# Forming 4-bit feed-forward weights during the attention, from gathered table rows

## The reference, cut to what matters

```python
def _dequant(qweight, scales, qzeros, g_idx):
    shifts = jnp.arange(PACK, dtype=jnp.uint32) * BITS            # PACK 8, BITS 4
    qw = qweight.astype(jnp.uint32)
    w = (qw[:, None, :] >> shifts[None, :, None] & MAXQ).reshape(-1, qweight.shape[1])
    qz = qzeros.astype(jnp.uint32)
    z = ((qz[:, :, None] >> shifts[None, None, :] & MAXQ) + 1).reshape(qzeros.shape[0], -1)
    s = scales[g_idx]
    return (w.astype(scales.dtype) - z[g_idx].astype(scales.dtype)) * s
Wg = _dequant(gate_qweight, ...)     # 512 x 1376, 4 groups
Wu = _dequant(up_qweight, ...)       # 512 x 1376, 4 groups
Wd = _dequant(down_qweight, ...)     # 1376 x 512, 10 groups
h = jax.nn.silu(xf @ Wg) * (xf @ Wu)
out = h @ Wd
```

## Time and profile before

| | us |
|---|---|
| median of 3 runs | 1183.19 (1180.73 to 1184.94) |
| the profiled execution, its time | 1182.78 |
| its span in the profile | 1181.0 |
| TensorE busy | 1121.7 (95%) |
| VectorE busy | 751.9 (64%) |
| ScalarE busy | 541.7 (46%) |
| GpSimd busy | 416.3 (35%) |

### The profile page before, as it was taken

One profiled execution on the slowest core, in us unless ns is written; L12 is line 12 of the kernel. 1 busy time (PEld: TensorE's weight loads), 2 busy tenths in 40 slices (PEclk: granted clock), 3 DMA queues, 4 the chain that ended last, 5 costly groups with the idle time before them and its releaser, 6 DMA issues. The chain is left out here.

```text
span 1181.0 us, 19222 instructions
## 1 busy us (share of the span) xinstructions
PE 1121.7 (95%) x6643; PEld 959.8 (81%) x6643; DVE 751.9 (64%) x1572; ACT 541.7 (46%) x1437; POOL 416.3 (35%) x421
## 2 busy tenths in 40 slices
PE   4899999999999999999999998789999999988998
PEld 3798998998998998998998887657768777676877
DVE  6555555555555555555555677789874566789863
ACT  4445445445445445445445454333332445465631
POOL 4442332332332332332332442144431333485521
PEclk9999999999999999999999999999999999999999
DMA  6211011011011011011010020023212225244300
GB/s 213 77 36 33 23 37 32 24 37 32 24 36 32 23 37 32 24 37 32 24 30 11 1 70 1 9 63 81 81 47 54 63 49 121 72 90 99 80 11 36
DMA packets 48716, 56.49 MB, mean 48 GB/s; under 512 B 10822, under 2 KB 29270, under 8 KB 48620
## 3 DMA queue, kind: packets, MB, share of 16 engines
q1 hardware_dynamic: 48620, 55.26, 17.3%
HBM read 40.56 MB, written 2.10 MB: 36 GB/s over the span
## 5 line engine op out<-in xcount | busy, mean ns | idle before, releaser
L379 PE MATMUL bank<-wqkv,kvT 128*128 128x256 f32 x1536 | 201.3, 288 | 8.7 <-DVE vv L567 8.7
L424 PE MATMUL bank<-wo,aoT 128*128 128x512 f32 x768 | 193.6, 401 | 5.6 <-DVE acc L563 5.6
L379 PEld LDWEIGHTS bank<-wqkv,kvT 128*128 128x128 f32 x1536 | 189.5, 193 | 10.4 <-DVE vv L567 10.4
L367 PE MATMUL bank<-wqkv,kvT 128*128 128x512 f32 x768 | 188.8, 395 | 1.7 <-DVE qn L577 1.7
L424 PEld LDWEIGHTS bank<-wo,aoT 128*128 128x128 f32 x768 | 140.6, 190 | 33.8 <-DVE aoT L558 6.3
L367 PEld LDWEIGHTS bank<-wqkv,kvT 128*128 128x128 f32 x768 | 141.7, 191 | 28.9 <-issue 1.8
L663 POOL TENSOR_TENSOR rms<-msq,half_neg 128x4 f32<-128x4 f32 x64 | 64.5, 1008 | 220.5 <-DVE msq L574 220.3
L666 POOL TENSOR_TENSOR rms<-msq,half_neg 128x2 f32<-128x2 f32 x64 | 44.6, 697 | 133.5 <-DVE msq L583 133.5
L550 ACT ACTIVATE prob<-bank,nmax 128x128 f32<-128x128 f32 x256 | 90.3, 372 | 2.1 <-DVE nmax L587 2.1
L875 PE MATMUL bank<-x2T,wgu 128*128 128x512 f32 (+1 forms) x336 | 90.3, 413 | 0.0
L528 ACT ACTIVATE qsq<-bank 128x512 f32<-128x512 f32 x64 | 38.2, 597 | 112.8 <-PE bank L367 112.8
(11 more groups left out here) (181 smaller groups left out, 2203.8 us busy)
## 6 DMA issues: line engine op xcount, KB each, us to landing
wqkv_raw<-in_L_xattn_Wq_dram SPq DMA_DIRECT2D x32, 256.0 KB, 2.5
wo_raw<-in_L_xattn_Wo_dram SPq DMA_DIRECT2D x32, 256.0 KB, 2.7
qS<-qhl SPq DMA_DIRECT2D x32, 256.0 KB, 3.7
kS<-chl SPq DMA_DIRECT2D x32, 128.0 KB, 3.1
packed<-_L_ffn_gate_qweight_dram SPq DMA_DIRECT2D x40, 64.0 KB, 2.3
packed<-in_L_ffn_up_qweight_dram SPq DMA_DIRECT2D x40, 64.0 KB, 2.3
packed<-_L_ffn_down_qweight_dram SPq DMA_DIRECT2D x10, 256.0 KB
acc<-in_x_dram SPq DMA_DIRECT2D x8, 256.0 KB, 5.7
```

What stands on the lines that cost most here:

```text
L367: mm = pe.matmul(b_q[:, :], kvT[:, l, kt, p, 1:3, :], wqkv[:, par, r, kt, 0:QW], start=(kt == 0 and n == 0), stop=(kt == KT - 1 and n == 2))
L379: mm = pe.matmul(b_kv[:, b * 256:(b + 1) * 256], kvT[:, l, kt, p, 2 * b:2 * b + 2, :], wqkv[:, par, r, kt, QW:QKV], start=(kt == 0 and n = ...
L424: mm = pe.matmul(b_o[:, :], aoT[:, l, h, :, :], wo[:, par, r, h, :], start=(h == 0 and n == 0), stop=(h == G - 1 and n == 2))
```

## The change

It takes dequantization out of the feed-forward part. Tables of zeros and scales are put together in DRAM (`sp_tables`, and the first three steps of `dve_between`): a row of `table[k, b]` has the zeros plus one and behind them the scales of one group, for up to 512 columns. The weights are cut into 35 chunks, [128 x 512] or [128 x 352] for gate and up and [128 x 512] for down. Each chunk is loaded by SP, with every packed row on 8 partitions; GpSimd gathers for each partition the table row of its group by an indirect DMA (`gather_row`, between the key power and `lo_piece`); VectorE forms the weights in three operations (`dequant`: shift and mask, subtract, multiply), in place; and SP stores them to DRAM. From step 5 on each step has two of these operations, one where `dve_between(..., "rq")` stands, between `msq` and `qn`, and one behind the step ("end").

In the feed-forward part a tile's weights are now loaded from DRAM (`weight_tile`, three tiles ahead), ScalarE makes the high part and VectorE (for tile 0 GpSimd) the low part, three operations of 512 columns each. The one-hot matrices, `spread`, the scale splits and everything that fed them are gone. The first products of the feed-forward part and the transposes of its input stand inside the last steps of the attention. Weight pieces of the attention are loaded in the same order as before, interleaved with the new loads and stores.

```diff
@@ sp_first
-            for g in range(1, KVH):
-                group(g)
-            sp_scales(sp)
-            wo_piece(KVH - 1, 3, 4 * KVH - 2)
+            qkv_piece(1, 0, 3)
+            wo_piece(0, 3, 2)
+            qkv_piece(1, 1, 4)
+            wo_piece(1, 0, 3)
+            sp_tables(sp)
+            for j in range(STEPS0 - 6):
+                sp_quantized(sp, j)
+                weight_load(j)
@@ pe_step0
+            if st.j == UNITS:
+                pe.wait_ge(s_qT, UNITS)
+                pe.wait_ge(s_kT, UNITS)
+                x2_transposes(pe, 0)
+                x2_transposes(pe, 1)
             if st.has(2, UNITS):
...
+            if st.j > UNITS and st.j < UNITS + 3:
+                inner_product(pe, 0, st.j - UNITS - 1)
             if st.has(3, UNITS):
...
+            if st.j == UNITS:
+                x2_transposes(pe, 2)
+                x2_transposes(pe, 3)
@@ dve_step0
                 dve.tensor_scalar(msq[:, 0:4], ssq[:, 0:4], 1.0 / HD, RMS_EPS, ALU.mult, ALU.add).then_inc(s_qms, 1)
+                dve_between(dve, st.j, "rq")
                 dve.wait_ge(s_rq, st.done(0))
@@ pool_step0
                 pool.tensor_tensor(rms[:, 4:6], msq[:, 4:6], half_neg[:, 4:6], ALU.pow).then_inc(s_rk, 1)
+            gather_row(pool, st.j)
             lo_piece(pool, st)
@@
+        FIRST = 5
+        BLOCKS = -(-F // D)
+        CHUNKS = 2 * KT * BLOCKS + FT
+        def weight_store(sp, c):
+            k, t, b, w, rows_, _ = chunk(c)
+            sp.wait_ge(s_deq, 3 * c + 3)
+            src = qch[0:rows_, c % 2, 0:w].bitcast(F32)
...
+        def sp_quantized(sp, j):
...
+            for c in range(CHUNKS):
+                if j == done_step(c) + 1 and c + 2 < CHUNKS:
+                    quantized_load(sp, c + 2)
+            for c in range(CHUNKS):
+                if j == done_step(c):
+                    weight_store(sp, c)
+        def done_step(c):
+            return FIRST + (3 * c + 2) // 2
+        def gather_row(pool, j):
+            for c in range(CHUNKS):
+                if j != (FIRST - 1 if c < 2 else done_step(c - 2)):
+                    continue
+                k, _, b, w, rows_, col = chunk(c)
...
+                if c >= 2:
+                    pool.wait_ge(s_deq, 3 * (c - 2) + 3)
+                pool.indirect_dma_start(rows[0:rows_, c % 2, 0:2 * w], None, table[k, b][:, :],
+                                        bass.IndirectOffsetOnAxis(idx[0:rows_, col:col + 1], 0)).then_inc(s_row[c % 2], 16)
@@ dve_between
+            if where in ("rq", "end"):
+                o = 2 * (j - FIRST) + (where == "end")
+                if 0 <= o < 3 * CHUNKS:
+                    dequant(dve, *divmod(o, 3))
+        def dequant(dve, c, step):
+            _, _, _, w, rows_, _ = chunk(c)
+            q = qch[0:rows_, c % 2, 0:w]
+            if step == 0:
...
+                dve.wait_ge(s_q_in[c % 2], 16 * (c // 2 + 1))
+                dve.tensor_scalar(q, q, shift[0:rows_, 0:1], 15, ALU.logical_shift_right, ALU.bitwise_and).then_inc(s_deq, 1)
+            elif step == 1:
+                dve.wait_ge(s_row[c % 2], 16 * (c // 2 + 1))
+                dve.wait_ge(s_deq, 3 * c + 1)
+                dve.tensor_tensor(q.bitcast(F32), q, rows[0:rows_, c % 2, 0:w], ALU.subtract).then_inc(s_deq, 1)
             else:
+                dve.wait_ge(s_deq, 3 * c + 2)
+                dve.tensor_tensor(q.bitcast(F32), q.bitcast(F32), rows[0:rows_, c % 2, w:2 * w], ALU.mult).then_inc(s_deq, 1)
@@ pe_ffn
             for n in range(FT + ALONE):
...
                 if n >= 1:
                     inner_product(pe, n, 0)
-                else:
-                    spread(pe, 1, (0, 1))
-                inner_product(pe, n, 1)
+                    inner_product(pe, n, 1)
@@ dve_ffn
                 if n + 1 < FT:
-                    dequant(dve, f + 1, (0, 1, 2))
+                    w_lo(dve, f + 1, (0, 1, 2) if n else (2,))
@@ sp_l1x
-            sp.wait_ge(s_zs, CHUNKS * FT)
+            sp.wait_ge(s_wqkv, 4 * KVH)
@@ the GpSimd block, ahead of the last step of ident
+            pool.memset(z_raw[:, :, :], 0).then_inc(s_blank, 1)
+            pool.memset(idx_raw[:, :], 0).then_inc(s_blank, 1)
+            pool.iota(pid[:, :], pattern=[[0, 1]], base=0, channel_multiplier=1).then_inc(s_pid, 1)
```

More of the change, by code:

```diff
@@ L703, in block_kernel @@
         f_d = bank[4:8]
[L704 to L707, removed]
+        FIRST = 5
+        WEIGHTS = (("gate", F, GG), ("up", F, GG), ("down", D, GD))
+        BLOCKS = -(-F // D)
+        CHUNKS = 2 * KT * BLOCKS + FT
+        z_line = [nc.dram_tensor(f"z_line_{m}", (g, n), F32).ap() for m, n, g in WEIGHTS]
+        w_gu = nc.dram_tensor("w_gu", (FT, P, 2, KT, P), F32).ap()
+        w_d = nc.dram_tensor("w_d", (F, D), F32).ap()
+        table = {(k, b): nc.dram_tensor(f"table_{m}_{b}", (g, 2 * min(D, n - b * D)), F32).ap()
+                 for k, (m, n, g) in enumerate(WEIGHTS) for b in range(-(-n // D))}
         ALONE = 3
         EVEN_DONE = UNITS - PAIRS
-        s_rest = sem("s_rest")
-        HALF_ZS, QUARTER_ZS = ZS // 2, ZS // 4
         X2 = 1
@@ L715, in width, with chunk @@
             return min(P, F - f * P)
-        def sp_scales(sp):
-            sp.wait_ge(s_zero, 1)
-            for m, at, n, g in TABLES:
-                for row in SCALE_ROWS:
-                    sp.dma_start(s_raw[row:row + g, at:at + n], a[f"L0_ffn_{m}_scales"]).then_inc(s_sraw, 16)
+        def chunk(c):
+            if c < 2 * KT * BLOCKS:
+                i, b = divmod(c, BLOCKS)
+                return i // KT, i % KT, b, min(D, F - b * D), P, i
+            f = c - 2 * KT * BLOCKS
+            return 2, f, 0, D, width(f), 2 * KT + f
@@ new lines, in stores, with stored, sp_tables @@
+        def stores(c):
+            return 1 + (c < 2 * KT * BLOCKS and c % BLOCKS == BLOCKS - 1)
+        def stored(c):
+            return 16 * sum(stores(b) for b in range(c % 2, c + 1, 2))
+        def sp_tables(sp):
+            sp.wait_ge(s_blank, 2)
+            for k, (m, n, g) in enumerate(WEIGHTS):
+                sp.dma_start(z_raw[0:g * n // 64, k, :], a[f"L0_ffn_{m}_qzeros"].rearrange("g c -> (g c)")
+                             .rearrange("(p c) -> p c", c=8)).then_inc(s_zraw, 16)
+                for b in range(-(-n // D)):
+                    w = min(D, n - b * D)
+                    sp.dma_start(table[k, b][:, w:2 * w], a[f"L0_ffn_{m}_scales"][:, b * D:b * D + w]).then_inc(s_tab, 16)
+            for k, m in enumerate(("gate", "up")):
+                sp.dma_start(idx_raw[:, k * KT:(k + 1) * KT],
+                             a[f"L0_ffn_{m}_g_idx"].rearrange("(t p) -> p t", p=P),
+                             allow_slow_non_contiguous=True).then_inc(s_idx, 16)
+            rest = F // P * P
+            sp.dma_start(idx_raw[:, 2 * KT:2 * KT + F // P],
+                         a["L0_ffn_down_g_idx"][0:rest].rearrange("(t p) -> p t", p=P),
+                         allow_slow_non_contiguous=True).then_inc(s_idx, 16)
+            sp.dma_start(idx_raw[0:F - rest, 2 * KT + F // P:2 * KT + FT],
+                         a["L0_ffn_down_g_idx"][rest:F].rearrange("(p o) -> p o", o=1)).then_inc(s_idx, 16)
@@ L858, in spread_next @@
-        def spread_next(pe, n, k):
-            if n + 1 < FT:
-                spread(pe, n + 1, (k,))
         def inner_product(pe, n, m):
@@ L900, in pe_ffn, with whole_down @@
         def pe_ffn(pe):
-            def whole_down(n, now):
-                down(pe, n, (0, 1))
-                spread_next(pe, now, 4)
-                down(pe, n, (2, 3)).then_inc(s_d, 1)
-                spread_next(pe, now, 5)
+            def whole_down(n):
+                down(pe, n, range(HP)).then_inc(s_d, 1)
             for n in range(FT + ALONE):
```

461 lines of the change are left out of this document (182 added, 279 removed).

## The result

The changed kernel takes 1142.88 us, the median of 4 runs (1142.49 to 1144.09), beside 1182.95 us (1180.73 to 1184.94) for the kernel before on the same chip. The ratio is 0.9662, with a 95% interval of 0.9646 to 0.9678. The forecast was 1146.0 us, in a range of 1138 to 1172. The profiled execution spans 1141.1 us, 39.9 less than the 1181.0 of before.

The account below looks back on a forecast made before the run. TensorE bounds attention without a gap; in FFN tiles table matmuls and waits for dequantization add 1.39 us to its 8.44. Sum: 1182.8 - 11.3 - 15.0 - 12.5 + 2.0 = 1146.0 us, range 1138 to 1172.

Parts of the forecast that it names:

- Attention's steps: Steps 5 to 57: the 105 new VectorE operations mostly fit idle time, 2.24 us at a step's end; cost 2 us.
- The rival of contention in every step: Attention: new operations meet GpSimd's low part and power every time, TensorE loses 0.5 us per step; 1170.5 us, chance 0.16.
- Table set-up: Steps 1 to 3 and before the first transpose: loads and 16 small VectorE operations lie in gaps; cost nothing.
- Steps 58 to 64: End of attention: zero tables, one-hots and scale splits of the old dequantization go; gain 11.3 us.
- Hand-over: Step 64's marker to tile 1's gate product: 23.5 us in place of 38.5; gain 15.0, ends 10 and 17.5.
- the spell at the lower clock: Hand-over: one spell of TensorE at a lower clock was expected to stay, 1.5 us of the 23.5.
- Tiles 1 to 10: FFN first half: only TensorE's 8.44 us per tile should bind, without the 1.39 us between; gain 12.5 us.
- The turn: Tile 10 to the second half of the FFN: the prediction had no term here, forecast change 0.
- The gather: 35 indirect DMAs on GpSimd in attention: about 4.2 us of GpSimd time free per gather, no loss taken.
- The 3.1 us that the prediction weighed against it: Gather: descriptors of a GpSimd DMA blocked by VectorE's two-port mode, from 620 to about 3100 ns; still below the threshold.
- the 7.5 us of the rival: Gather too long: query power late, then TensorE; loss above 4.2 us, break-even 6.4, at 7.5 us 1202; chance 0.11.

Follow-up runs that it names:

- the second of the edits: The changed kernel with the VectorE operation at the step's end moved ahead of the queries, in front of the square sums: 1141.99 us, ratio 0.9653.
- the trace at 4.0 us: The changed kernel with 9 chained small memsets behind each gather, so that GpSimd is held for 4.0 us: 1156.35 us, ratio 0.9761.
- 18 memsets: The changed kernel with 18 chained small memsets on GpSimd behind each gather, so that it is held for 7.2 us: 1238.38 us, ratio 1.0465.

## Why the prediction was right, and where it was not

The sum came out 3.1 us above the median: 39.9 us of span were gained, and 36.8 forecast. No single term made that difference. The two stretches missed by more than 2 us have opposite signs and nearly cancel; what is left is the hand-over, and a little of each of the others. That the sum came so close owes 2.5 us each way to luck.

**Attention's steps, +2.0 forecast, +1.33 measured.** The mechanism was the one named: the operation at the end is held by GpSimd's low part, and in a step without a gather the excess over the room reaches TensorE. 0.18 us per event was right (0.2). The number of events was not worked out; there are 6. Moving the operation away, the second of the edits above, removed the loss in every step. The rival of contention in every step, 1170.5 us, is excluded: 35 operations are stretched and 27 of them cost nothing.

By the rule of the Trainium skill that the prediction weighed ("SBUF — State Buffer", section "Who interferes with whom"), the two-input operations are held for the whole of GpSimd's instruction; the trace agrees, at 2.35 us. The prediction took the rule for two-input operations alone; line 1062, with one tensor input and a scalar per partition, was held in the same way, 2.10 us.

**Table set-up, nothing forecast, +2.1 measured.** This step failed. It was called a matter of gaps "of the same kind", and the step's end has room for 2.24 us; but in steps 1 and 2 the first of four small shifts was held by GpSimd's low part, 1.25 and 1.86 us in place of 0.17. The four took 1.49 and 2.09 us together, and TensorE waited 1.60 us for `vv` in place of 0.22, and in the next step 0.45 in place of nothing. The room at the end of an early step was not read from a row of that step; the rows were from 300 us on. The version with the set-up ahead of the queries has these 2.1 us back. Another 0.45 us are in the start before the first marker, which varies by more from run to run (41.5 to 43.7 us in the profiles here).

**Steps 58 to 64, -11.3 forecast, -11.6 measured.** As argued; no run takes this term apart.

**Hand-over, -15.0 forecast, -16.6 measured.** The windows of the kernel before and, in the second fence, of the changed one, over exactly this stretch:

```profile
745.65:784.14 38.49, 26.61 (x132) 20.37 (x131) 29.68 (x69) 12.99 (x32) 9.41 (x14) 0.91 0.11 28
```

```profile
737.93:759.81 21.88, 20.09 (x113) 16.90 (x112) 17.00 (x33) 12.56 (x28) 6.21 (x7) 1.00 0.12 37
```

TensorE's own work is 20.09 us, where the sum had 19.4. The wait for `qT` is 1.20, as forecast, and one more of 0.59 is left where the sum had 1.3; these two misses cancel. The term that failed is the spell at the lower clock, 1.5 us: the clock is 1.00 throughout, with stops of 1.20 and 0.59 us and no longer one. Before, TensorE stood idle for 11.9 us of the stretch, and the clock was 0.91 in it.

**Tiles 1 to 10, -12.5 forecast, -12.7 measured.** The first takes 8.98 us, with a wait of 0.41 for `hval`; the others take 8.35, a little less than the 8.44 that gate, up and down take in the earlier trace rows. VectorE's 3.5 us per tile were near: 9.55 us in three tiles, 3.2 each. The prediction put the 1.39 us on the table matmuls and on waiting for the dequantization together and did not say which. The run without the table matmuls does: they alone give 0.47 per tile, and then VectorE, at 95%, is the bound.

**The turn, nothing forecast, -2.65 measured.** A step that is missing from the prediction. The two waits for `xn` were in the trace of before, behind the earlier trace rows, and the diff widens their buffer; with the early normalization taken back, 2.45 us return.

**The gather.** Right in what it does: 1.03 us of GpSimd, and no loss. The Trainium skill ("DMA: Bandwidth & Descriptors", section "Latency and other measured facts") has about 1 us up to the first byte of a DMA from GpSimd; the trace's 1.03 us, the time for which a gather holds GpSimd, is close to that. The 3.1 us that the prediction weighed against it did not occur: the longest gather held GpSimd for 1.22. Wrong in how far the slack reaches. The prediction added the idle times and `pT`'s slack up to 4.2 us and put 17 us of loss on each microsecond beyond, with a break-even at 6.4. The runs show no loss at 2.7, 12 us in the steps at 4.0, and a break-even near 5. In the trace at 4.0 us the slack behind the power is shared with the operation at the step's end, and beyond it TensorE not only stops, it is slow afterwards (granted clock 0.72 from 330 to 336 us with 18 memsets). At the 7.5 us of the rival the price was 1202; at 7.2 it is 1238.

**Not settled.** Where the 0.2 us between 2.45 and 2.65 at the turn go, and what the profiled run with the late normalization lost in the second half (its span is 5.2 us longer than that of the changed kernel, of which the turn explains 2.45; it was the slowest of its four runs). From the second half's first gate to the end it took 294.1 us, where the changed kernel took 291.2 and 292.9 in its two profiles and the second of the edits 294.2, so this lies within what this stretch varies by from run to run.

## What to carry to other kernels

An idle time of VectorE can be filled only as far as GpSimd leaves it alone: put work where GpSimd is idle or doing something short (here ahead of the queries), not where its long two-input instruction starts. Read the room from a row of each kind of step that gets work, the first ones of a loop too. In this kernel slacks along one chain could not be added up, where another new operation took its share of them; and before a stage is priced, look at the engine next to the bound, which here would have kept 1.0 of the 1.5 us per tile.

## What the runs showed of the hardware that was not expected

- A VectorE operation with a scalar per partition and one tensor input was held by GpSimd's two-input operation as well: 2.10 us against 0.48 for line 1062, and 1.86 against 0.17 for a shift with constants on 96x24. Where nothing holds it (the second of the edits), line 1062 takes 0.48 us on 512 columns and 0.40 on 352, the subtraction 0.69 and 0.52: 0.5 ns per column against 1.0, worked out from these. So the one-input operation that is held is one that runs at twice the rate.
- An indirect DMA of up to 128 rows held GpSimd for 0.95 to 1.22 us and landed 3.8 to 5.4 us after its issue.
- GpSimd's power on 128x4 takes 1.01 us alone and up to 1.42 beside a VectorE operation (309.49 above), so the holding goes both ways.
- After a stop of 3.00 us the six matmuls of line 433 took 1.65 us in place of 0.88, in a window with a granted clock of 0.72; after stops of 1.83 and 2.10 us, 3.7 us apart, twelve of line 416 took 4.57 us in place of 2.9 at 0.63; after stops of 1.20 us and less in the hand-over the clock stayed at 1.00.
